# Column strips for the state products, column halves for the dt projection and the aux products, in a fused Mamba-2 block with FP4 feed-forward

## The reference, cut to what matters

```python
zxbcdt = u @ in_proj_w.T                      # z 1024, x 1024, B 128, C 128, dt 64 heads
dt = softplus(dt_raw + dt_bias);  dA = dt * -exp(A_log)
# per chunk of 64 tokens, head h (64 heads of 16 features), state size 128:
Y_diag = einsum('bzcn,bzsn,bzhcs,bzshp->bzchp', Cc, Bc, L, Xdt)
state  = state * chunk_decay + einsum('bzcn,bzch,bzchp->bzhpn', Bc, decay_states, Xdt)
Y_off  = einsum('bzcn,bzhpn,bzch->bzchp', Cc, state_before, exp(dA_cum))
```

## Time and profile before

| | |
|---|---|
| median of 3 runs | 1783.25 us (1782.76 to 1784.73) |
| the profiled execution | 1782.91 us, span in the trace 1781.1 us |
| mean granted PE clock | 0.971 of full speed |
| PE busy | 1626.2 us of the span (91%) |
| DVE, POOL, ACT busy | 1304.0, 1119.5, 930.2 us |
| L850, the 896 passes of `from_before` | 114.0 us busy |
| L819 and L820, 128 and 64 passes | 21.9 and 19.9 us busy |
| L770 with 64 columns of weights, 96 passes | 39.6 us busy |
| L1062 gb x128 on ACT, L989 dta x16 | 40.7 us, 9.0 us busy |

### The profile page before, as it was taken

The page is one execution under the profiler, slowest core; times in us unless marked ns, Lnnn a source line. Parts: engine busy times, 40 slices in busy tenths (PEclk is TensorE's granted clock), DMA queues, the critical chain, the costliest instruction groups (busy, mean ns, idle before and its releaser), DMA issues.

```text
span 1781.1 us, 36900 instructions
## 1 busy us (share of the span) xinstructions
PE 1626.2 (91%) x11168; PEld 818.8 (46%) x11168; DVE 1304.0 (73%) x2016; ACT 930.2 (52%) x1647; POOL 1119.5 (63%) x1087
## 2 busy tenths in 40 slices
PE   2699999989998998998998998888999999999998
PEld 1245545535544544544554554543344444444443
DVE  5939858858867876975985886656777777777774
ACT  2454454354445445435436436325766666666662
POOL 0038738837936845863873882885777776667773
PEclk9889999999999998998999999888999999999999
DMA  6121151141133124014114115721111101101011
GB/s 228 46 57 29 27 120 45 23 107 52 28 76 91 24 56 113 17 45 120 29 27 114 52 23 117 195 27 48 36 47 38 60 29 55 54 30 60 24 36 60
DMA packets 214697, 109.81 MB, mean 62 GB/s; under 512 B 133796, under 2 KB 185696, under 8 KB 214496
## 3 DMA queue, kind: packets, MB, share of 16 engines
q1 hardware_dynamic: 214496, 107.37, 22.5%
HBM read 80.57 MB, written 26.76 MB: 60 GB/s over the span
## 4 chain that ended last, share of the span: by engine, by line
PE 54%; issue 14%; DVE 12%; POOL 11%; ACT 4%; DMA 1%; SPq 1%; DVEq 0%; POOLq 0%; ACTq 0%
PE ps_in L770 12%; PE ps_in L924 8%; PE ps_yo L939 6%; PE ps_yd L939 6%; PE ps_in L792 6%; PE ps_s L924 4%; PE ps_t L924 4%; POOL xend L1665 4%; DVE pre L1270 3%; POOL y L1685 2%; PE ps_yo L850 2%; POOL y L1679 2%; DVE mix L1358 2%; PE ps_yd L840 1%; POOL sq L1702 1%
## 5 line engine op out<-in xcount | busy, mean ns | idle before, releaser
L770 PE MATMUL ps_in<-u_hi,w_hi 128*128 128x512 f16 (+1 forms) x608 | 234.3, 385 | 60.6 <-DVE u_lo L1257 32.4
L1665 POOL TENSOR_TENSOR xend<-xpad,decay 128x256 f32<-128x256 f32 x256 | 223.8, 894 | 102.9 <-PE ps_yo L863 47.1
L1075 ACT ACTIVATE decay<-ps_d 128x512 f32<-128x512 f32 x256 | 149.5, 592 | 243.6 <-PE ps_d L828 151.6
L792 PE MATMUL ps_in<-w_out,zg 128*128 128x512 f32 x512 | 230.8, 604 | 3.0 <-DVE pre L1270 2.5
L770 PE MATMUL ps_in<-u_lo,w_hi 128*128 128x512 f16 (+1 forms) x608 | 233.5, 384 | 0.0
L770 PE MATMUL ps_in<-u_hi,w_lo 128*128 128x512 f16 (+1 forms) x608 | 233.2, 383 | 0.0
L1358 DVE TENSOR_TENSOR mix<-decay,gb 128x1024 f32<-128x1024 f32 x128 | 179.3, 1401 | 49.3 <-ACT decay L1075 35.1
L1763 POOL TENSOR_TENSOR gate_sum<-gate_sum,gate_part 128x512 f32<-128x512 f32 x88 | 142.2, 1616 | 104.4 <-DVE gate_part L1586 104.0
L1270 DVE SCALAR_TENSOR_TENSOR pre<-ps_in,cws,pre 128x511 f32<-128x511 f32 (+2 forms) x240 | 179.2, 747 | 14.4 <-ACT pre L1014 8.1
L792 PEld LDWEIGHTS ps_in<-w_out,zg 128*128 128x128 f32 x512 | 95.8, 192 | 134.7 <-issue 124.2
L924 PE MATMUL ps_in<-xt_hi,gu_w 128*128 128x512 f16 x352 | 134.4, 382 | 5.5 <-DVE gate_sum L1586 2.3
(11 more groups left out here) (181 smaller groups left out, 3732.3 us busy)
## 6 DMA issues: line engine op xcount, KB each, us to landing
ebc<-e_dram SPq DMA_DIRECT2D x256, 64.0 KB, 2.7
u<-u_t SPq DMA_DIRECT2D x9, 1024.0 KB, 4.9
res<-u_tok SPq DMA_DIRECT2D x32, 256.0 KB, 3.7
x_dram<-res SPq DMA_DIRECT2D x32, 256.0 KB, 2.1
xa<-x_dram SPq DMA_DIRECT2D x8, 1024.0 KB, 5.8
xr<-x_dram SPq DMA_DIRECT2D x32, 256.0 KB, 2.6
out<-xr SPq DMA_DIRECT2D x32, 256.0 KB, 2.1
fw_words<-gu_words SPq DMA_DIRECT2D x32, 176.0 KB, 4.4
```

Of the source, the lines that this page charges most:

```text
L770: last = mm(ps_in[bk][0:m, :], w[:, k, col:col + m], u[:, k, :], start=(k == 0 and j == 0), stop=(k == KT - 1 and j == 2))
L792: last = mm(ps_in[bk][:, :], zg[:, k, tt * P:(tt + 1) * P], w_out[:, k, :], start=(k == 0), stop=(k == CT - 1))
L1075: ac(decay[:, n % NG, :, :].rearrange("p a b -> p (a b)"), ps_d[n % 2][:, :], ACT.Exp).then_inc(e_done, 1)
L1665: g_.tensor_tensor(xend[:, pairs, :], xpad[:, c % 2, pairs, :], decay[:, g, :, CH - 1:CH].broadcast_to([P, CT, 2 * HD]), ALU.mult).then_in ...
```

## The change

`from_before` gives each of its eight products to four column strips: 32 columns of the state as weights, the same 64 columns of C, at tile positions 0, 32, 64 and 96. The dt projection is done in two column halves: the first 256 tokens into partitions 0 to 63 and the others into 64 to 127 of the bank, 24 products in place of 12; the bias lies twice in dtbias (one more small transfer at the start), and `take_dt` is one operation on 128 partitions. The products of B and C are made twice, into both halves of the partitions, and so is the transposed B, now as an fp32 product with the identity in place of a transpose; ACT copies gb in one operation.

```diff
-        dtbias = sb("dtbias", [NH, 1])
+        dtbias = sb("dtbias", [P, 1])
-        N_SMALL, N_CONST = 16 * 5, 16 * 17
+        N_SMALL, N_CONST = 16 * 6, 16 * 17
-                     (dtbias[:, :], dt_bias), (aneg[:, :], a_log)]
+                     (dtbias[0:NH, :], dt_bias), (dtbias[NH:2 * NH, :], dt_bias), (aneg[:, :], a_log)]
...
+                if name == "dt":
+                    for k in range(KT):
+                        for j, (w, u) in enumerate(passes):
+                            for h in range(2):
+                                last = mm(ps_in[bk][h * NH:(h + 1) * NH, 0:LH], w[:, k, col:col + NH],
+                                          u[:, k, h * LH:(h + 1) * LH], start=(k == 0 and j == 0),
+                                          stop=(k == KT - 1 and j == 2), tile_position=(0, h * NH))
+                    last.then_inc(in_full[bk], 1)
+                    return
...
-                    mm(ps_t[0:CH, 0:CH], bc[:, 0, t], bc[:, 1, t], start=True, stop=True)
-                    last = tr(ps_t[0:CH, CH:CH + NS], bc[:, 0, t], ident[:, :])
+                    for h2 in range(2):
+                        mm(ps_t[h2 * CH:(h2 + 1) * CH, 0:CH], bc[:, 0, t], bc[:, 1, t], start=True, stop=True,
+                           tile_position=(0, h2 * CH))
+                    for h2 in range(2):
+                        last = mm(ps_t[h2 * CH:(h2 + 1) * CH, CH:CH + NS], bc[:, 0, t], ident[:, :],
+                                  start=True, stop=True, tile_position=(0, h2 * CH))
...
-                    last = mm(ps_yo[:, k * CH:(k + 1) * CH], state[:, k * P:(k + 1) * P],
-                              bc[:, 1, c * CH:(c + 1) * CH], start=True, stop=True)
+                    for strip in range(NG):
+                        rows = slice(strip * 32, (strip + 1) * 32)
+                        last = mm(ps_yo[rows, k * CH:(k + 1) * CH], state[:, k * P + strip * 32:k * P + (strip + 1) * 32],
+                                  bc[:, 1, c * CH:(c + 1) * CH], start=True, stop=True, tile_position=(0, strip * 32))
...
-                for h in range(2):
-                    last = ac(dta[h * NH:(h + 1) * NH, :], ps_in[bk][0:NH, h * LH:(h + 1) * LH], ACT.Identity,
-                              bias=dtbias[:, 0:1], scale=uundo[0:NH, 0:1])
-                last.then_inc(in_free[bk], 1)
+                ac(dta[:, :], ps_in[bk][:, 0:LH], ACT.Identity, bias=dtbias[:, 0:1], scale=uundo[:, 0:1])\
+                    .then_inc(in_free[bk], 1)
...
-                    for h2 in range(2):
-                        last = ac(gb[h2 * CH:(h2 + 1) * CH, c % 2, :], ps_t[0:CH, 0:CH + NS], ACT.Copy)
+                    last = ac(gb[:, c % 2, :], ps_t[:, 0:CH + NS], ACT.Copy)
```

More of the change, by code:

```diff
@@ L765, in project @@
                 need(pe, in_free[bk], free)
-                col, m = IN_COL[name], (NH if name == "dt" else P)
+                col = IN_COL[name]
                 passes = [(w_hi, u_hi), (w_hi, u_lo), (w_lo, u_hi)]
+                if name == "dt":
[7 more added lines that the diff above has]
+                    return
                 for k in range(KT):
                     for j, (w, u) in enumerate(passes):
-                        last = mm(ps_in[bk][0:m, :], w[:, k, col:col + m], u[:, k, :],
+                        last = mm(ps_in[bk][:, :], w[:, k, col:col + P], u[:, k, :],
                                   start=(k == 0 and j == 0), stop=(k == KT - 1 and j == 2))
```

## The result

The changed kernel takes 1741.5 us (median of 4 runs, 1740.6 to 1742.5) against 1784.0 us before on the same chip: ratio 0.9759, interval 0.9743 to 0.9774. That is 42.5 us, where 1760 us, some 24 us less than before, was forecast. The profiled execution took 1741.6 us with a span of 1739.8, so the span fell by 41.3 us.

A forecast was written before the change was run, and what follows sets the result against it. PE bounds up to chunk 1 and from late chunk 6; DVE and POOL cover between. Seven bodies at 2.7 (18.9), last body 3.3, prologue 1.2: 23.4 us saved, 1760 us; own range 1750 to 1766, whole 1738 to 1774.

The forecast's parts named there:

- rival (a): Gain comes in all chunks because the DVE stretch is not stiff: 24 us more, 1736 us; chance 0.2.
- I take 0.7: State products on PE: 64 strip passes at 18 ns save 0.7 us a chunk; bounds 0.2 to 0.9.
- Nothing in chunks 2 to 5 and in chunk 6: Faster state products save nothing there: DVE's own work covers chunks 2 to 5, POOL's xend chunk 6.
- The floor that I weighed: Matmul starts at least 25 ns apart: state products would save 0.24 us, whole forecast some 9 us higher.
- dt: dt projection on PE, slot 4: two overlapping halves save 1.2 us a body, 1.2 in the prologue; ends 1.35 and 0.
- ACT's single copy: One ACT copy of gb instead of two, showing on the chain at slot 2: saves 0.3 us a body.
- Aux: Aux products on PE in halves: 0.06 us longer per group, counted as 0.2 us a body lost.
- At the loop's turn none is busy: Loop's turn, 534 to 541 us: next body waits for ACT; the change touches nothing there, no saving counted.
- a period below 138: Sign in the loop body's period, forecast 139.8 us from 142.5: below 138 means the gain comes in all chunks.
- (b): dt halves do not overlap, or POOL and ACT take over in chunk 1: 9.6 us less saved, 1770; chance 0.14.
- (c): State products, every chunk: the four strips do not overlap, kernel some 115 us slower, to 1900; chance 0.05.
- (d): DVE and POOL meet the gain at once everywhere: time stays within 3.6 us of 1783; chance 0.04.

The follow-up runs named there:

- all edits, stop kept: Changed kernel with 24 semaphore increments on ACT ahead of its loop, otherwise the same: 1753.2 us, ratio 0.9803.

## Why the prediction was right or wrong

The measured 1741.5 us lies below the forecast's own range, 1750 to 1766. It lies in the whole range, 1738 to 1774, only because that took in most of rival (a), which did not happen. That part is luck: a cause that neither had gave 11 to 15 us.

**The state products** were right in kind and, as a step, a little small. The step "I take 0.7" measured 0.93 in chunk 1 and 1.05 over chunks 5 to 7, at the better end of its bounds, as it would be if 96 strip passes in a row pay for the change of shape once: the 32 of `within` now take 0.47 us to the next start for 0.58. "Nothing in chunks 2 to 5 and in chunk 6" held in the loop: 57.13 against 57.04 us, and the kernel with strips in two chunks alone. The forecast's 9.8 us for chunks 1 and 7 and its 3.6 in the last body make 13.4; taking the strips out of the changed kernel cost 13, putting them into the kernel before gave 22 (14 to 25).

**The floor that I weighed.** The Trainium skill, TensorE: Matmul & The Clock Gate, section "Wait — 56ns, not 53.3ns?", says that matmuls never start closer than about 25 ns. That is not what these passes do: 1.02 us for 64 is 16 ns. The measurement decides.

**dt** was sized well as a step: 1.28 us for 1.2. Its halves overlap. The prologue gave 2.05 us for 1.2: the chain has dt and B together at 8.02 us before, 24 passes from 32.37, and at 2.77 + 3.20 = 5.97 after. The clock rose earlier too, by the length of the passes: 12 passes of B took 3.20 us here, and 2.6 is what they take at 2.4 GHz throughout. The forecast's 9.6 us for dt came out as 5 to 7 in the time.

**ACT's single copy**, 0.3 us a body, was a mis-sized term: two copies cost nothing measurable. **Aux** at +0.06 was 0.49 for 0.50, so the 0.2 a body counted for it did not come either.

**The step that failed** is a sentence, not a term: "At the loop's turn none is busy: the next body waits for ACT to come round, and nothing of the change touches that." I saw the idle stretch in the earlier trace rows, named the engine, and did not ask why ACT took so long. It stood still for 4 us with nothing to wait for, and the change moved it: ahead of the loop ACT has two instructions fewer from dt and nine from the copies of gb, so its loop begins 11 earlier, and it is 9 shorter. That was worth about 11 us by medians (1753.2 against 1742.6 on one chip), 14.9 in the spans, 13.7 in the kernel before by itself (1786.1 against 1772.4).

By place the span adds up so, in us saved against before; the forecast's terms are sorted in by where it put them:

| place | forecast | all edits, stop kept | changed |
|---|---|---|---|
| start to the yoff of chunk 1 in the first body | 3.2 | 3.7 | 4.2 |
| yoff of chunk 1 to chunk 7, seven bodies | 4.9 | 6.7 | 6.7 |
| yoff of chunk 7 to chunk 1 of the next body, seven times | 12.0 | 14.1 | 28.4 |
| last body, chunk 1 to 7 | 3.3 | 3.0 | 2.3 |
| the rest, with the feed-forward part | 0 | -1.0 | -0.3 |
| together | 23.4 | 26.4 | 41.3 |

The two kernels part in one row, that of the turns. The single edits on one chip add up by medians too: strips 21.8, dt 7.4, aux and copy 0.4, stop 13.7, together 43.3 for the 42.5 measured. So the edits gave 26 to 35 us for the 23.4 forecast and the stop 11 to 15, by which kernels are set side by side; closer than that the runs do not split it.

**The rivals.** (a) is refuted for the loop, although its number, 1736, lies nearer than mine. My own test would have misled me: "a period below 138 would speak for (a)". The period is 136.2, and the gain lies where neither put it. A period cannot say in which part of the body time was saved. (b) is out too: the halves overlap. Its second half came true without the price: POOL's wait for yoff in chunk 1 is gone, so POOL is level with DVE there, and the gain still passed: the stretch into the loop is 2.4 us shorter, dt's 1.3 and the strips' 0.9. (c) and (d) are out by the passes and the time.

**Why the stop comes and goes.** ACT's loop in each kernel, counted in the trace's records of ACT from one branch back to the next, with where it begins against the kernel before:

| kernel | length | begins | ACT's stop | q14 packets |
|---|---|---|---|---|
| before; strips only | 310 | 0 | yes | 104 |
| dt only | 309 | -2 | no | 79 |
| aux only; changed with old dt | 302 | -9 | no | 81; 80 |
| changed; with old products or in part | 301 | -11 | no | 80 |
| changed, moved by 16 | 301 | +5 | no | 81 |
| changed, moved by 24 | 301 | +13 | yes | 104 |
| before, moved by 56 | 310 | +56 | no | 80 |
| changed, two copies, moved by 60 | 309 | +58 | no | 80 |

One rule fits all of these: instructions come in blocks of 128, and ACT stops at a taken branch when its loop touches four of them, not when it touches three (384 instructions at most). The loop of before must then begin 75 to 77 into a block (75 + 310 = 385 is too long, and dt only, 77 - 2 + 309 = 384, just fits). With that, 24 more ends at 389 or later, 16 more by 383, and 56 or 58 more begin anew in the next block. The moved-by-16 kernel was written from this and came out so. Loops that cannot fit in 384 stop wherever they lie: ACT's second loop is 429 long and stops in every kernel here, and so does DVE's, 387 long. The chain that ended last, at ACT's second loop, and DVE's timeline, after:

```profile
1430.95 3.25 issue
```

```profile
380.87 1.55 DVE L1370 TENSOR_TENSOR mix<-decay,gb 128x1024 f32<-128x1024 f32 x1 [3.15 <-issue]
```

DVE's falls while the z tiles run, and behind it DVE waits for ACT twice (1.22 and 0.78 us), so this stop is not on the path. ACT's first loop stops where PE, DVE and POOL wait for ACT. Its second loop's stop is on the chain, once in every kernel.

The places in the table alone would allow two blocks of 256 as well as three of 128: a loop that begins 203 to 205 into a block of 256 gives the same yes and no in every row. What decides is when q14's packets come, one by one, in the trace of before, in the code that an engine runs straight through. A packet starts within 1 us after the start of 10 of the 13 DVE records whose number (each loop counted once) is 64 above a multiple of 128, of 6 of the 11 ACT records so placed, and of all 6 SP records that are 80 above one; over all places it is 5 to 7 in 100. Taken as the step into a new block, this puts the beginning of ACT's loop 76 into one, within the 75 to 77 that the table asks for. It also puts DVE's loop of 387 at 35, so it ends at 422 and stops, and SP's of 356 at 17, so it ends at 373; SP stands still for 0.29 us at its branch. The reading of the packets as block steps is an inference, but place, length and stop agree on three engines.

The Trainium skill, Runtime: NRT & Kernel Launch, section "Instruction fetch mechanics", says that a taken branch to a target outside the window that is held must fetch it first. That agrees with the stops. Its window of two blocks of 256 does not: the packets here are of 8.2 KB, half the size it names, they come every 128 records, and the limit seen is three of them.

**The clock took a share.** In the six stretches from chunk 7 to chunk 1 of the next body the mean granted clock was 0.92 to 0.94 before and 0.94 to 1.00 after. A mean below 1 is some us at 1.2 GHz, and they come behind the gap in which PE has nothing to do at the turn. In the moved kernel with the stop it is back at 0.91 to 0.94. So part of what the stop costs may be paid at the lower clock, after it is over; no kernel here separates the two. It also makes the same stretch differ by a microsecond or two from kernel to kernel and from body to body, which may be why dt's share came out small; that was not settled.

## What to carry to other kernels

An engine that stands idle behind its branch with no semaphore to wait for is a cost of its own: look for "<-issue" of some microseconds at each turn of a loop, and check whether the loop can be shortened or moved by a few instructions before its arithmetic is touched. The label alone proves nothing: POOL, with a loop of 238, stands at the same turn with

```profile
389.03 1.96 POOL L1679 TENSOR_TENSOR y<-xs,dskip 128x512 f32<-128x512 f32 x1 [7.04 <-issue]
```

in the kernel before, yet the next record of POOL follows 0.08 us behind the branch, and after the change it is 6.82. The packets of q14 and a kernel that only moves the loop tell the two apart. When an edit changes the number of instructions ahead of or in a loop, run it once more with padding ahead of the loop, or its effect and that of the place can't be told apart. And where a stretch is idle, write down what ends the idleness before calling it untouched.

## What the runs showed of the hardware

- At a taken branch ACT stood still for 2.9 to 4.4 us in its first loop, and DVE for some 3 us where the loop touched more than three blocks of 128 instructions; where ACT's did not, its next record came 0.2 us behind the branch. The same code, moved by 56 instructions, ran 13.7 us faster (8 to 18).
- 64 fp32 strip passes of 64 columns that read the same moving tile started 16 ns apart on average; the 32 of `within`, whose strips read four, took 15 ns each right ahead of them and 18 before the change.
- Two column halves of dt, 24 passes of 256 columns, took 1.43 us where 12 of 512 took 2.71, 0.53 of the time.
- With DVE's 24 taps of a stretch at 6.8 us for 17.9, DVE's busy time fell by only 1.6 us, as other operations of it became longer (dtb 2.24 us for 0.85).
- At the turns PE's idle time was followed by a fall of the granted clock; the kernels without the stop had less of it.
